# 46 transposes whose output nobody reads around the token lists, and the row of ones filled by VectorE, in a one-core transformer with routed experts

## The reference

```python
h = _L0_tok_ref(x, L0_tok_weight, L0_tok_move_bias)
h = concatenate([h, txt], axis=1)
h = h + _L0_attn_ref(_layernorm(h), ...)
h = h + _L0_ffn_ref(_layernorm(h), ...)
h = h + _L1_attn_ref(_layernorm(h), ...)
h = h + _L1_ffn_ref(_layernorm(h), ...)

def _L1_ffn_ref(x, Wr, W1, b1, W2, b2):
    topw, topi = top_k(x_flat @ Wr, 2)
    topw = softmax(topw)
    combine = zeros((T, 8)).at[arange(T)[:, None], topi].add(topw)
    h = relu(einsum('td,edh->eth', x_flat, W1) + b1[:, None, :])
    y = einsum('eth,ehd->etd', h, W2) + b2[:, None, :]
    return einsum('te,etd->td', combine, y)
```

## Time and profile before

| what | us |
|---|---|
| median of 3 runs | 987.47 |
| lowest and highest of them | 986.82, 988.18 |
| the profiled execution, its own time | 987.98 |
| its span, first to last instruction | 986.2 |
| TensorE busy in the span | 796.1 (81%) |

### The profile page before, as it was taken

One profiled execution on the slowest core, in us unless ns is written; L12 is line 12 of the kernel. 1 busy time (PEld: TensorE's weight loads), 2 busy tenths in 40 slices (PEclk: granted clock), 3 DMA queues, 4 the chain that ended last, 5 costly groups with the idle time before them and its releaser, 6 DMA issues. The chain is left out here.

```text
span 986.2 us, 22686 instructions
## 1 busy us (share of the span) xinstructions
PE 796.1 (81%) x7550; PEld 657.6 (67%) x7551; DVE 546.0 (55%) x1512; ACT 437.8 (44%) x1056; POOL 297.3 (30%) x310
## 2 busy tenths in 40 slices
PE   3489999999779866556566999973289999999993
PEld 2378888888669533233343788852189999999993
DVE  1727777777775121111163666758446666666662
ACT  4446666676443311111002698746234444444441
POOL 1321121110023000000200478720165655555552
PEclk9759999999975687877785999985579999999997
DMA  9393000000000599999707400008713332323331
GB/s 275 84 418 149 2 0 0 0 0 1 1 2 2 196 427 426 425 425 426 283 20 282 203 1 1 0 2 148 120 39 58 49 54 47 54 50 48 55 49 20
DMA packets 39274, 119.31 MB, mean 121 GB/s; under 512 B 10739, under 2 KB 29653, under 8 KB 34805
## 3 DMA queue, kind: packets, MB, share of 16 engines
q1 hardware_dynamic: 28120, 105.62, 29.3%
q0 software_dynamic: 10848, 12.76, 8.0%
q10 hardware_dynamic: 244, 0.14, 0.1%
HBM read 105.70 MB, written 12.56 MB: 120 GB/s over the span
## 5 line engine op out<-in xcount | busy, mean ns | idle before, releaser
L1731 POOL DMA_INDIRECT out_h<-x_ys,idx x55 | 87.2, 1585 | 98.7 <-ACT x_ys L1757 84.3
L1863 PE MATMUL psum<-w_pairs,x_h_hi 128*128 x330 | 102.1, 371 | 1.1 <-DVE x_h_lo L1791 1.1
L1865 PE MATMUL psum<-w_pairs,x_h_lo 128*128 x330 | 82.7, 251 | 0.0
L1791 DVE TENSOR_TENSOR x_h_lo<-psum,x_h_hi 128x384 fp32r<-128x384 f32 x110 | 56.3, 553 | 41.6 <-ACT x_h_hi L1752 41.5
L1757 ACT ACTIVATE x_ys<-x_ys,x_cw 128x192 f32<-128x192 f32 x55 | 25.1, 457 | 99.0 <-DVE x_ys L1802 99.0
L1752 ACT ACTIVATE x_h_hi<-psum 128x384 fp32r<-128x384 f32 x110 | 48.1, 488 | 40.4 <-PE psum L1852 40.3
L1863 PEld LDWEIGHTS psum<-w_pairs,x_h_hi 128*128 128x128 f32 x330 | 61.9, 188 | 3.0 <-issue 3.0
L1865 PEld LDWEIGHTS psum<-w_pairs,x_h_lo 128*128 128x128 f32 x330 | 62.9, 191 | 0.0
L1105 PE MATMUL psum<-flat,m_yT 64*32 64x384 f32 x576 | 39.3, 637 | 29.0 <-issue 27.7
L1718 POOL DMA_INDIRECT x_xg<-xtab,idx x55 | 55.1, 1002 | 16.6 <-issue 16.3
L478 POOL TENSOR_SCALAR a_xn<-flat,rstd,nmr 96x192 f32<-96x192 f32 x32 | 16.0, 499 | 136.6 <-PE psum L609 136.5
(11 more groups left out here) (290 smaller groups left out, 2227.1 us busy)
## 6 DMA issues: line engine op xcount, KB each, us to landing
flat<-in_slot_w SPq DMA_DIRECT2D x24, 2304.0 KB, 28.7
flat<-in_moe_w SPq DMA_DIRECT2D x1, 10752.0 KB, 29.0
ring_last<-in_slot_w SPq DMA_DIRECT2D x4, 2304.0 KB, 34.1
m_y<-in_slot_w SPq DMA_DIRECT2D x4, 2304.0 KB, 31.2
flat<-in_x_patches SPq DMA_DIRECT2D x4, 1536.0 KB, 15.7
out_h<-flat SPq DMA_DIRECT2D x1, 2304.0 KB, 12.3
xtab<-flat SPq DMA_DIRECT2D x4, 576.0 KB, 10.7
ytab<-f_y2g SPq DMA_DIRECT2D x7, 192.0 KB, 35.3
```

Source lines behind the costliest of these rows:

```text
L1731: pool.indirect_dma_start(out=A["out"][:, :], out_offset=bass.IndirectOffsetOnAxis(ap=g.idx[:, i:i + 1], axis=0), in_=ys[:, i % 2, :], in_ ...
L1791: v.tensor_tensor(h_lo[:, 3 * n:3 * n + 3, :], b_hT[n], h_hi[:, 3 * n:3 * n + 3, :].bitcast(F32), ALU.subtract).then_inc(s_hl, 1)
L1863: pe.matmul(b_y[u % 2], h_hi[:, k, :], g.w_pairs[:, :, k, bass.ds(e, 1), :].rearrange("p two a d -> p two (a d)"), start=(k == 0), stop=False)
L1865: mm = pe.matmul(b_y[u % 2][:, 1, :], h_lo[:, k, :], g.w_pairs[:, 1, k, bass.ds(e, 1), :].rearrange("p a d -> p (a d)"), start=False, stop ...
```

## The change

TensorE gets 34 transposes of the identity matrix at the end of its part of `route`, behind the last token list, and 12 more at the start of its part of `expert_tiles`, ahead of every wait there. They write bank 7 of PSUM, which no later instruction of these two blocks reads. The fill of `one` and its copy into `x_lo` move from the head of GpSimd's list to the head of VectorE's; GpSimd's wait for its own copy goes away.

```diff
                 mm.then_inc(s_list if q == NP - 1 else s_part, 1)
+            for _ in range(34):
+                pe.transpose(g.ps[:, 7, 0:128], g.ident[:, :], g.ident[:, :])
...
         @block.gpsimd
         def _(pool):
-            pool.memset(one[:, :], 1.0).then_inc(s_mem, 1)
-            pool.wait_ge(s_mem, 1)
-            pool.tensor_copy(x_lo[64:128, 1, :], one[64:128, :]).then_inc(s_one, 1)
-            pool.wait_ge(s_one, 1)
             for t in range(NTILES + 4):
...
         @block.vector
         def _(v):
+            v.memset(one[:, :], 1.0).then_inc(s_mem, 1)
+            v.wait_ge(s_mem, 1)
+            v.tensor_copy(x_lo[64:128, 1, :], one[64:128, :]).then_inc(s_one, 1)
             for n in on_vector:
...
         @block.tensor
         def _(pe):
+            for _ in range(12):
+                pe.transpose(g.ps[:, 7, 0:128], g.ident[:, :], g.ident[:, :])
             pe.wait_ge(s_one, 1)
```

## The result

| | before | changed |
|---|---|---|
| median of 12 runs each, taken by turns | 990.42 us (986.82 to 994.02) | 995.24 us (992.42 to 1000.2) |
| ratio | | 1.0065, 95% interval 1.0043 to 1.0087 |
| profiled execution: own time, span, clock | 987.98, 986.2, 0.865 | 1000.2, 998.4, 0.854 |

The change makes the kernel slower by 0.65%. The forecast (986.6 us, 985.3 to 988.3, "the same") was wrong in sign and in range. Its 986.6 stood on a median of 987.47 for the kernel before, which came out at 990.42 over these 12 runs, so 3.0 us of the distance to 995.24 are the level of the runs. What the forecast has to answer for is the difference: 0.9 us faster was forecast, 4.8 us slower was measured.

A forecast was written before the change was run, and what follows sets the result against it. TensorE was taken to set the pace of the expert tiles, so earlier gains arrive whole. 987.98 − 1.27 (earlier gather) + 0.35 (lost beside `b2`) = 987.06, 0.51 lower as a median: 986.6 us, range 985.3 to 988.3.

The forecast's parts named there:

- VectorE's fill and copy … Cost 0: Start of expert tiles: the moved operations take 0.6 us, leaving 0.8 us of cover before `x_lo` is asked for; cost 0.
- What is next in line: Before `second(0)`: GpSimd's late pieces end at 725.3, TensorE arrives at 726.15, so they don't bind but cap any gain.
- A microsecond gained before `second(0)` … should arrive whole at the end: Expert tiles from 727.07: they run at TensorE's pace, so earlier gains reach the kernel's end in full.
- 1.27 us gained: Head of expert tiles: without GpSimd's fill and copy the first gather is issued 1.27 us sooner, bounds 1.14 and 1.42.
- VectorE's operations beside the issue, 0 with a bound of 0.5: First gather's issue: VectorE's two small operations beside it make no difference, at most 0.5 us.
- 0.35 lost beside `b2`: First gather's landing: its packets may wait behind those of `b2`, 0 to 0.75 us; the middle, 0.35, taken.
- Twelve transposes, 0: Start of expert tiles: twelve at 0.25 us take 3.0 us, hidden under the gather with 0.8 us left; cost 0.
- 34 transposes, 0: End of `route`: 34 take 8.6 us, ending at 706.0, before ScalarE ends at 711.61; cost 0.
- The cap: GpSimd's late pieces end at 725.3 after the change; nothing can bring `second(0)` ahead of that.
- Clock, 0: TensorE's clock at the tiles' start: still 0.50, rising as far behind the first product as before; effect 0.
- the first rival: Clock up for tile 0 or rising some microseconds sooner: 0.85 us more gain, 985.7 us; chance 0.17.
- Slower: Rival: transposes dearer than 0.25 us, delaying the block's end and first transposes; 3.0 us slower, 990.5 us; chance 0.06.

The follow-up runs named there:

- early_pieces: Kernel before, with GpSimd's four late pieces issued after its third gather instead of its fourth; `x_mine` ended with the first piece, a piece lasting 1.79 us.
- move_only: Changed kernel without the transposes, only fill and copy moved to VectorE; median 992.12 us, ratio to before 1.0068.
- act_fill: `move_only` without VectorE's two operations, ScalarE writing the row of ones; `second(0)` 18.4 us behind the block's start.
- guard: Changed kernel, with GpSimd waiting for `s_cw` at 1 between its fourth gather and its late pieces; median 986.08 us, ratio to before 1.0010.
- best: `gm_pad6` again, timed in rounds; 987.32 us against 987.51 before, ratio 0.9991.
- act_guard: `act_fill` with the wait of `guard` ahead of GpSimd's late pieces; median 987.06 us against 987.25 before, ratio 0.9999.
- gm_pad6: `move_only` with the wait of `guard` and six one-column memsets on VectorE at the end of `route`; single run 983.6 us against 985.7.
- gm_pad14: `move_only` with the wait of `guard` and 14 one-column memsets on VectorE at the end of `route`; single run 982.4 us against 985.7.
- before_pad3: Kernel before, with three one-column memsets on VectorE at the end of `route`, its list two longer; third tile of a pass 4.58 us, 4.45 before.
- tr_only: Kernel before with only the 34 and 12 transposes added, fill and copy left on GpSimd; median 986.39 us, ratio 1.0012.
- hold: `move_only` with GpSimd waiting for VectorE's first late piece ahead of its first gather; `x_cw` 7.68 us, `second(0)` 20.1 us behind the block's start.
- before_ppad2: Kernel before, with two one-column memsets on GpSimd at the end of `route`; `second(0)` 14.5 us behind the block's start.
- again: The changed kernel once more, timed in rounds; median 990.72 us, ratio to before 1.0058.

## Why the prediction was wrong

**The step that failed first is "VectorE's fill and copy … Cost 0" with "What is next in line".** It asked of GpSimd's four pieces only when TensorE needs them, and of VectorE only whether it is free by 716.9. It never asked whom the pieces keep out. `x_mine` and `x_cw` stand on VectorE between the pieces and the relu, read two operands from SBUF each, and are asked for just where GpSimd passes from a gather to the pieces. The trace of before had a warning. Its group of L1777 (nanoseconds min/median/max) and the longest one in the timeline:

```profile
L1777 DVE TENSOR_TENSOR x_mine<-x_xg,tef x55: 140/149/839, 718.3 to 966.8; 128x1 f32<-128x1 f32 x55
725.33 0.84 DVE L1777 TENSOR_TENSOR x_mine<-x_xg,tef 128x1 f32<-128x1 f32 x1
```

It is tile 1's, begun inside the last piece and ended with it (726.17, the piece 726.15). It cost nothing there, so I hadn't looked. A wait for a single piece can be read from that row; a wait for four can't. The Trainium skill ("SBUF — State Buffer", on the port that VectorE and GpSimd share) describes a lock that lasts for a whole instruction; `early_pieces` agrees (1.37 us, to the end of the piece), the hang of 7.1 to 7.8 us over four instructions goes beyond it.

**What is shown and what isn't.** Shown: taking the work from GpSimd brings the hang, whichever engine gets it (`move_only`, `act_fill`); the hang needs the pieces behind the gather with no wait for `x_cw(0)` between (`guard`, `best`, `act_guard`, `gm_pad6`, `gm_pad14`); it costs 4 us of `second(0)` through the relu. Excluded as its cause: the transposes, VectorE's two operations, the moment at which `x_mine` is asked for, the time of the first gather, the place in GpSimd's list. Open: what GpSimd's own fill and copy do that keeps the later hang away. That the pieces stand ready behind the gather isn't enough for a hang: in before, the wait at L1717 for the next gather, which stands behind the pieces in GpSimd's list, is met at 718.7, 0.3 us before the first piece starts, so GpSimd had read its list past the pieces by then, and nothing hangs. GpSimd's fill without its own wait for the copy was not tried.

**"A microsecond gained before `second(0)` … should arrive whole at the end"** failed too. `guard` gained 1.2 us there against the profile of before (0.5 against the usual) and lost more in the tiles: VectorE's loop sits two instructions further on, 1.7 us (`before_pad3`). The sum had no term for it. For `guard` 0.5 gained and 1.7 lost make a ratio of 1.0012; measured is 1.0010. The two together, 4.0 + 1.7 = 5.7 us, are 0.58% of 987, and 0.65% with the 4.7 of the usual case; measured are 0.58%, 0.65% and 0.68%.

**Terms of the sum that were mis-sized.** *1.27 us gained*: 0.65. The first gather starts 0.78 us behind the block's start (predicted 0.16, before 1.43), in `act_fill` at 0.77, so a pause that I put down to GpSimd's two operations belongs to the gather. *VectorE's operations beside the issue, 0 with a bound of 0.5*: 0.21. The issue takes 1.66 us, before 1.45. In `act_fill` it takes 1.15, so against an issue without these operations they cost 0.51. *0.35 lost beside `b2`*: 0.13. From the end of the issue to the first transposes it is 2.02 us, before 1.89; in `act_fill`, whose issue ends 0.5 us sooner, it is 2.58, near the bound of 0.75. Together 0.65 − 0.21 − 0.13 leaves 0.3 us of gain at the first transposes (4.46 against 4.77 behind the start), where 0.9 stood.

**What held.** *Twelve transposes, 0*: 2.79 us, over at 720.82, 1.6 us before the gather lands. *34 transposes, 0*: over at 707.3, ScalarE starts its last work 4.5 us later and ends 10.4 later; `tr_only` times them. *The cap*: without GpSimd's fill and copy the pieces end 13.7 to 13.9 us behind the start except in `act_fill` (13.25) and `hold` (14.6); predicted was 13.4. Where the hang is gone they bind, by 0.6 us in `best` and 1.2 in `guard`. "So they don't bind" was read from the one profile of before, in which the clock rose late; in `before_ppad2` they bind by 0.8. The wait of TensorE in `guard`, 725 to 735 us:

```profile
PE psum L1867 <- POOL w_pairs L1724: 1.2, 1, 1.2
```

*Clock, 0*: 0.50 at the first product of the changed kernel. But one reason under it was wrong: "Nor do transposes look like work that raises the clock". They do, here at 706.2, 5.3 us behind the start of the 34, and in `again`, `tr_only` and `guard` 5.1, 4.9 and 3.6 behind it. In the 16 profiles without the 34 the clock does not rise there. In `guard` the clock was up once more behind the twelve, which are TensorE's only work from 703.1 to 715.8 (windows of `guard`, columns as in the earlier trace rows):

```profile
711.40:714.20 2.80, 2.76 (x12) 2.35 (x12) 2.72 (x5) 0.00 (x0) 1.80 (x2) 0.50 0.69 228
714.80:718.10 3.30, 1.13 (x6) 0.90 (x7) 1.40 (x5) 0.38 (x1) 2.67 (x4) 1.00 0.33 101
718.20:721.50 3.30, 2.98 (x11) 2.52 (x11) 0.82 (x3) 0.88 (x2) 3.30 (x2) 0.50 0.15 40
```

The first product, at 717.41, there ran at 1.00 for 0.7 us, which is the first rival in small; the pieces took what it gained, as the cap says. The other three profiles with the twelve don't show it. The mixture of the earlier trace rows misled me, and the rule that the prediction cites from the Trainium skill ("TensorE: Matmul & The Clock Gate", its part on PE transpose) does not hold in this trace; what kept the changed kernel's first product at 0.50 was the hole behind the 34.

**The rivals.** "Slower" named the right sign with the wrong mechanism: the transposes were cheaper than 0.25 us (2.79 / 12 = 0.23 at the low clock, 6.47 / 34 = 0.19 with the clock raised for a part), not dearer. The last rival, a rise fixed on the time axis, and the forecast's "as far behind the first product as before" both took the rise in one profile for a constant. Over the profiles that don't hang it comes 9.8 to 14.6 us behind the start, and 3.2 to 8.0 behind the first product.

## What to carry to other kernels

When an operation leaves an engine, look at what its neighbours on other engines now meet: list the operations of VectorE with two SBUF operands near GpSimd's long ones, and read the *longest* of each group beside the median. If TensorE waits for VectorE and the row it waits for is short, look at the row ahead of it in VectorE's order; a semaphore wait that lets the small operation in before GpSimd's long ones took the hang away here. When a difference of 0.2% in a looped kernel must be explained, compare also the pause behind the branch, and pad the list before giving a change the credit or the blame.

## What the runs showed that I had not expected

- One VectorE operation on 128 elements took 7.1 to 7.8 us, over four GpSimd operations of 1.79 us, though it got in at the first border when it was asked for inside one.
- The same loop on VectorE pauses 0.41, 0.51 or 0.63 us from its branch to the relu (in each profile nine passes agree within 0.02 us), by whether the list ahead is longer by 7 or 15, by 0 or 1, or by 2 instructions.
- Transposes took the granted clock from 0.50 to 1.00: the 34 in 4 of 4 profiles, the twelve alone in 1 of 4.
- In profiles without a hang the clock rises between 9.8 and 14.6 us behind the block's start, which alone moves `second(0)` by 0.7 us.
